# Attention with a causal mask, 1 core: the second key block masked by GpSimd on the probabilities, its PV one slot later

## The chip, the cores and the metric

One Trainium2 chip, one core. The metric is the device time of one launch in microseconds. The engines are TensorE (PE; its weight loads are PEld), VectorE (DVE), ScalarE (ACT), GpSimd (POOL) and SyncE (SP, which issues DMAs).

## The reference

```python
xn = _layernorm(x)                         # x: 32 x 256 x 128, float32
x = x + attention_block(xn) + expert_layer(xn)
# in the attention block, 16 heads of 8:
scores = jnp.einsum('bhse,bhte->bhst', Q, K) * scale
scores = jnp.where(causal[None, None], scores, -1000000000.0)
attn = jax.nn.softmax(scores, axis=-1)
ctx = jnp.einsum('bhst,bhtd->bhsd', attn, V)
```

The attention block goes on with a low-rank output projection, a residual, a second layer norm and a low-rank GELU MLP. The expert layer routes each token to 2 of 9 experts (SiLU gate, width 352). Only the causal mask and the product with V are touched by the change.

## The kernel before

**Stages.** 8192 tokens are 16 chunks of 512, which is 2 sequences of 256 each. A first stage loads and normalises x and makes the router's logits. The second stage, 16 steps of attention, one chunk in each, runs from about 86 us to 588 us of the span. The third stage does the experts and the MLP. The change is in the second.

**A step.** Each engine has its own `step(half, d)`, an order written out by hand over 24 slots (`2 * UNITS`, `UNITS` = 12). A slot does one score unit. Slots 0 to 11 are the chunk's first sequence (b = 0), 12 to 23 the second (b = 1). In a half chunk, units u = 0 to 7 are the scores of the first 128 keys against 256 queries, 2 heads in each, and units 8 to 11 those of the last 128 keys against the last 128 queries, 4 heads in each; both are 128 keys on the partitions by 512 columns. The first keys against the last queries need no mask; the diagonal blocks do.

**A slot.** PE makes the scores with one matmul (`score_unit`, L1057), whose contraction has a 97th row: the negated row maximum of each query is in the stacked queries, so the result is already score minus maximum. A second matmul (L1058) adds `mask_ts` (0 or -1e30) to the diagonal blocks through the identity: 256 columns in units 0 to 7, all 512 in units 8 to 11. It ends with `scores_done`. ACT takes the exp of it (`exp_unit`, L846) from PSUM into one of 8 SBUF buffers `probs` and ends with `exp_done`. PE then multiplies two units' probabilities with V (`probs_times_v`, called PV below; L1075 for units below 8, L1082 for the others); PV number n takes units 2n and 2n + 1, 12 of them in a chunk. In each slot PE also does one max unit (`max_unit`, L1034 and L1037): the same scores with queries on the partitions, for a later half chunk, of which DVE takes the row maxima (L1441).

**The row maxima's way.** In slot 9 (for b = 1) and in slot 21 (for the next chunk's b = 0) PE turns the maxima (`turn_max`, L1090), ACT negates them into `neg_max` (`copy_max`, L839), and SP puts them by DMA into the 97th row of the stacked queries (`stack_max`, L486). The score of slot 12, or of slot 0 of the next chunk, is the first that reads them, and PE waits there:

```python
if u == 0:
    pe.wait_ge(max_stacked[b], 16 * (c.index + 1))
```

**Where PV stands.** In slots 3, 5, ... 23 PE does PV 0 to 10 after the slot's score and mask; PV 11 comes in slot 1 of the next chunk. In each slot the order is: score, mask, PV if any, the other small products (projections of q, k and v in slots 12, 14 and 2, the context's turns and output projection in 6, 8, 10, 18, 20, 22, the turn of the maxima in 9 and 21), then the max unit. After the last chunk PV 11 stands alone.

**POOL.** Its `step` goes over 12 pairs of slots. In pair k it waits until the scores of slot 2k are done (`after_scores`) and then issues, as the case may be, one row scatter of 128 tokens by an indirect DMA (L664; from chunk 3 on, in pairs 0 to 9, from chunk 11 on in pairs 0 to 11), a part of the key stack (L626; pairs 1 to 3 and 8 to 10), expert weights (pairs 0 and 6, eight chunks), and in pair 7 the output bias onto xn (L649). In the last chunk it also splits expert weights (L704). POOL doesn't take part in the scores.

**Buffers.** Two PSUM banks take the scores in turn: the score of slot m waits for the exp of slot m - 2. The exp of an even slot m waits for the PV that read the same `probs` buffers 8 units before.

Of the kernel before, what the change touches and what calls it, by code (L numbers as in the profile page):

```python
# [34 lines left out]
P = 128  # L35
# [24 lines left out]
def at(half, d):  # L60

    return Step(2 * half + d, d % 2, half + d // 2)
# [99 lines left out]
def first_and_attention(nc, env):  # L162
# [18 lines left out]
    with ExitStack() as stack:  # L181
# [160 lines left out]
        max_scores, max_taken = s.sem("max_scores"), s.sem("max_taken")  # L342
        max_turned, max_copied = s.sem("max_turned"), s.sem("max_copied")
        max_stacked = s.two_sems("max_stacked")
        scores_done, exp_done = s.sem("scores_done"), s.sem("exp_done")
        pv_done, ctx_copied = s.sem("pv_done"), s.sem("ctx_copied")
        ctx_back, inv_ready, ctx_ready = s.sem("ctx_back"), s.sem("inv_ready"), s.sem("ctx_ready")
        ctx_again, ctx_turned_ready = s.sem("ctx_again"), s.sem("ctx_turned_ready")
# [32 lines left out]
        def scatter_at(step, pair):  # L381

            if pair < ROWS_OF.get(step, 0):
                j = ROWS_AT[step] + pair
                return j // (2 * TPC), j % (2 * TPC)
            return None

        def fill_at(step, pair):

            if pair < 2 * TPC and step < LATE:  # L390
                k = 2 * TPC * step + pair
                return k if k < FILLS else None
            return None
# [13 lines left out]
        SPLIT_PAIRS = range(1, 1 + EXPERTS)  # L407
        SPLIT_SLOTS = range(4, 4 + 2 * EXPERTS, 2)
        HALVES = 2 * UNITS // 2


        Q_AT, K_AT, V_AT = (1, 9), (2, 10), 4
# [12 lines left out]
        with nc.Block() as block:  # L425
# [138 lines left out]
            def _(pool):  # L564
# [97 lines left out]
                def scatter(c, col):  # L662
                    t, k = divmod(col, 2)
                    pool.indirect_dma_start(env["slot_x"][:], bass.IndirectOffsetOnAxis(ap=slot_now[c.parity][:, col:col + 1], axis=0),  # L664
                                            xs[c.parity][:, t, k, :], None).then_inc(scattered[c.parity], 16)

                def after_scores(p, slot):
                    pool.wait_ge(scores_done, 2 * UNITS * p.index + slot)
                    pool.sem_inc(scatter_started, 1)

                def step(half, d):
                    p = at(half, d)
                    x = p.index
                    last = x == last_chunk
                    two_ahead = x < last_chunk - 1
                    for pair in range(HALVES):
                        after_scores(p, 2 * pair + 1)
                        rows, blank_part, weights = scatter_at(x, pair), fill_at(x, pair), weights_at(x, pair)
                        if x == LATE and pair == 0:
                            pool.wait_ge(slots_ready, 1)  # L680
                            pool.wait_ge(zero_filled, 16 * FILLS)
                            pool.wait_ge(routed_all, 1)
                        if rows is not None:
                            if rows[1] == 0:
                                number_rows(at(0, rows[0]))
                            scatter(at(0, rows[0]), rows[1])
                        if blank_part is not None:
                            fill(blank_part)
                        if pair == BIAS_AT:
                            add_bias(p)  # L690
                        if pair in K_SECOND_AT and not last:
                            stack_k_part(at(half, d + 1), 1, K_SECOND_AT.index(pair))
                        if pair in K_FIRST_AT and two_ahead:
                            if pair == K_FIRST_AT[0]:
                                pool.wait_ge(k_split, x + 3)
                                pool.sem_inc(k_stack_started, 1)
                            stack_k_part(at(half, d + 2), 0, K_FIRST_AT.index(pair))
                        if weights is not None:
                            load_weights(weights)
                        if last and pair in SPLIT_PAIRS:  # L700
                            pool.wait_ge(experts_loaded, 16 * W_LOADS)
                            pool.sem_inc(scatter_started, 1)
                            e = SPLIT_PAIRS.index(pair)
                            pool.tensor_copy(w_hi[:, e, :], w_gate_up[:, e, :].bitcast(F32)).then_inc(w_hi_ready, 1)  # L704
# [201 lines left out]
            def _(pe):  # L906
# [133 lines left out]
                def score_unit(c, m):  # L1040
# [13 lines left out]
                        g = u - 8  # L1054
                        keys, queries, lanes = k[rows, g, hi:end], slice(hi, end), slice(0, LANES)
                    by_lane = ps[:].rearrange("p (i s) -> p i s", s=queries.stop - queries.start)
                    pe.matmul(by_lane, keys, q[rows, g, lanes, queries], start=True, stop=False, skip_group_check=True)  # L1057
                    pe.matmul(by_lane[:, :, 0:P], ident_b[:], mask_ts[:, lanes, :], start=False, stop=True, skip_group_check=True).then_inc(scores_done, 1)  # L1058

                def probs_times_v(c, n):  # L1060

                    b, u = divmod(n, HALVES // 2)
                    seq = 2 * c.index + b
                    pe.wait_ge(exp_done, 2 * UNITS * c.index + 2 * (n + 1))
                    if n == 0:
                        pe.wait_ge(v_ready, c.index + 1)
                    if u == 0 and seq == 3:
# [48 lines left out]
                def step(half, d):  # L1116
# [4 lines left out]
                    before, here = 2 * x - 1, 2 * x  # L1121
                    for slot in range(2 * UNITS):
                        score_unit(p, slot)
                        if slot % 2 == 1 and slot >= 3:
                            probs_times_v(p, (slot - 3) // 2)
                        if slot == 1 and not first:
                            probs_times_v(at(half, d - 1), HALVES - 1)
                        if slot == 2 and not last:
                            project_v(nxt, bank_of(0, d), max_copied, 2 * x + 1)
                        if slot == COUNT_AT and x == 1:  # L1130
# [87 lines left out]
                step(chunks // 2 - 2, 1)  # L1218
                step(chunks // 2 - 1, 0)
                step(chunks // 2 - 1, 1)  # L1220
                probs_times_v(at(chunks // 2 - 1, 1), HALVES - 1)
                end = 2 * chunks - 1
                keep_busy(m_ps[0], 3)
                context_back(end, bank_of(1, 2), h_done, end)
# [862 lines left out]
```

## Time and profile before

| | us |
|---|---|
| median of 3 runs | 999.45 |
| lowest, highest | 994.67, 1008.21 |
| the profiled execution | 1002.02 |
| its span, first to last instruction | 1000.1 |
| mean granted TensorE clock in it | 0.982 |

The durations in the profile are from that one execution; the difference between 1002.02 and 1000.1 lies around the span. A matmul's row gives its start and a modelled end, and matmuls are pipelined, so what one costs PE is read from the starts, its own and the next one's. A PEld row is a weight load, which overlaps the matmul before it. The text in brackets behind a row is the idle time of that engine ahead of it and what ended it.

### The profile page before, as it was taken

The numbers are of one execution on the slowest core, as the hardware profiler recorded it, in microseconds if no ns is written. First come the engines' busy times: TensorE is split into PE (matmuls) and PEld (weight loads), VectorE is DVE, ScalarE is ACT, GpSimd is POOL, SyncE is SP. The second block draws the span as 40 slices with busy tenths as digits, with TensorE's granted clock in tenths as the row PEclk, the third lists the DMA queues.
The fourth block names the chain that finished last, engine by engine and source line by source line (L and its number), as shares of the span: only waits on it lengthen the run. The fifth ranks groups of instructions, "written<-read, shape, count | busy, mean of one in ns | idle before, by whom it ended". The sixth has DMA issues, their size and how long they took to land. (4 is left out here: it accounts for less than half of the span.)

```text
span 1000.1 us, 25308 instructions
## 1 busy us (share of the span) xinstructions
PE 956.2 (96%) x7722; PEld 742.4 (74%) x7722; DVE 698.5 (70%) x3195; ACT 533.9 (53%) x1248; POOL 428.1 (43%) x557
## 2 busy tenths in 40 slices
PE   4689999999999999999999989999999999999997
PEld 4455666666666666666666659999999999989896
DVE  5768889778777777777777745555555554558887
ACT  2663555555555555555555555555555555564442
POOL 9331221354645556454555425444444444430110
PEclk8779999999999999999999999999999999999999
DMA  9477453444554454443433032222222222248874
GB/s 243 126 233 228 164 206 110 136 137 132 156 150 131 126 151 141 130 121 105 134 107 121 30 90 72 66 66 62 66 64 65 65 65 65 73 135 232 230 214 135
DMA packets 139765, 127.12 MB, mean 127 GB/s; under 512 B 17338, under 2 KB 121908, under 8 KB 139636
## 3 DMA queue, kind: packets, MB, share of 16 engines
q1 hardware_dynamic: 116336, 68.94, 25.4%
q0 software_dynamic: 20592, 56.43, 18.0%
q8 instruction: 67, 1.10, 0.5%
q10 hardware_dynamic: 2708, 0.15, 0.2%
q14 instruction: 62, 0.51, 0.2%
HBM read 57.15 MB, written 42.60 MB: 100 GB/s over the span
## 5 line engine op out<-in xcount | busy, mean ns | idle before, releaser
L1441 DVE CUSTOM_DVE_ANT_0 att_masked_st<-att_m_ps,att_mask_st 128x128 bf16<-128x128 f32 (+1 forms) x1024 | 311.4, 353 | 100.1 <-PE att_m_ps L1034 52.1
L846 ACT ACTIVATE att_probs<-att_t_ps 128x512 f32<-128x512 f32 x384 | 229.0, 597 | 206.2 <-PE att_t_ps L1058 201.0
L1683 POOL DMA_INDIRECT y_scratch<-moe_y,moe_row_now x136 | 131.6, 968 | 153.8 <-DVE moe_y L1937 112.6
L664 POOL DMA_INDIRECT slot_x<-xs,att_slot_now x128 | 127.7, 998 | 151.3 <-PE att_t_ps L1058 128.4
L1931 DVE TENSOR_TENSOR moe_hidden<-moe_gate,moe_up_ps 128x352 f32<-128x352 f32 x136 | 70.9, 521 | 109.8 <-ACT moe_gate L1858 108.1
L1058 PE MATMUL att_t_ps<-att_mask_ts,att_ident_b 128*128 128x256 bf16 (+1 forms) x384 | 122.9, 320 | 0.0
L1760 PE MATMUL moe_y_ps<-w_down,moe_hidden_t 128*128 (+1 forms) x816 | 114.0, 276 | 1.7 <-DVE moe_y L1937 1.5
L1858 ACT ACTIVATE moe_gate<-moe_gate_ps 128x352 f32<-128x352 f32 x136 | 63.1, 464 | 97.2 <-PE moe_up_ps L1743 97.2
L1760 PEld LDWEIGHTS moe_y_ps<-w_down,moe_hidden_t 128*128 128x128 f32 (+1 forms) x816 | 101.8, 191 | 3.5 <-issue 3.2
L1441 DVE DVE_READ_ACCUMULATOR2_ANT att_row_max<- 128x1 f32 x1024 | 84.5, 83 | 0.1
L1057 PE MATMUL att_t_ps<-even_stack,att_k_stack 97*128 97x512 f32 x192 | 80.5, 419 | 3.6 <-DMA even_stack<-att_neg_max 3.2
L1057 PE MATMUL att_t_ps<-att_odd_stack,att_k_stack 97*128 97x512 f32 x192 | 80.9, 423 | 2.4 <-DMA att_odd_stack<-att_neg_max 2.4
L1058 PEld LDWEIGHTS att_t_ps<-att_mask_ts,att_ident_b 128*128 128x128 bf16 x384 | 37.3, 97 | 60.4 <-issue 52.1
L1075 PE MATMUL att_pv_ps<-att_probs,att_v_ones 128*32 128x256 f32 x1024 | 81.8, 391 | 0.0
L626 POOL DMA_DIRECT2D att_k_stack<-att_qk_parts x96 | 55.8, 581 | 30.9 <-PE att_t_ps L1058 28.4
L1034 PE MATMUL att_m_ps<-att_k_stack,even_stack 96*128 96x256 f32 x256 | 66.6, 342 | 2.4 <-DMA even_stack<-att_qk_parts 1.4
L1752 PE MATMUL moe_hidden_ps<-ident,moe_hidden 128*128 128x128 f32 (+1 forms) x408 | 66.7, 272 | 0.0
L1034 PE MATMUL att_m_ps<-att_k_stack,att_odd_stack 96*128 96x256 f32 x256 | 65.1, 336 | 0.6 <-DVE att_row_max L1441 0.6
L1743 PE MATMUL moe_gate_ps<-even_stack,moe_x_lo 128*128 x136 | 55.6, 409 | 0.7 <-DVE moe_x_lo L1925 0.7
L1034 PEld LDWEIGHTS att_m_ps<-att_k_stack,even_stack 96*128 96x128 f32 x256 | 40.0, 193 | 20.9 <-issue 18.1
L1852 ACT CAST moe_x_hi<-moe_x_ps 128x128 fp32r<-128x128 f32 x136 | 36.1, 267 | 33.2 <-PE moe_x_ps L1724 33.2
L1752 PEld LDWEIGHTS moe_hidden_ps<-ident,moe_hidden 128*128 128x128 f32 (+1 forms) x408 | 51.0, 136 | 2.9 <-issue 0.2
(268 smaller groups left out, 2053.6 us busy)
## 6 DMA issues: line engine op xcount, KB each, us to landing
att_k_stack<-att_qk_parts POOLq DMA_DIRECT2D x96, 128.0 KB, 3.3
slot_x<-xs POOLq DMA_DIRECT2D x17, 516.0 KB, 3.5
xs<-slot_x SPq DMA_DIRECT2D x34, 258.0 KB, 3.0
xs<-xn_scratch SPq DMA_DIRECT2D x32, 256.0 KB
mlp_rows<-y_scratch POOLq DMA_DIRECT2D x16, 512.0 KB, 5.4
even_stack<-att_qk_parts SPq DMA_DIRECT2D x192, 32.0 KB
att_odd_stack<-att_qk_parts SPq DMA_DIRECT2D x192, 32.0 KB
first_words<-in_L_attn_hidden_states SPq DMA_DIRECT2D x8, 512.0 KB, 7.9
```

The source lines that it names most:

```text
L664: pool.indirect_dma_start(env["slot_x"][:], bass.IndirectOffsetOnAxis(ap=slot_now[c.parity][:, col:col + 1], axis=0), xs[c.parity][:, t, k ...
L846: act.activation(probs[:, m % PT, :], t_ps[m % 2][:], ACT.Exp).then_inc(exp_done, 1)
L1034: last = pe.matmul(ps[:, n * SEQ:(n + 1) * SEQ], q[0:ROWS, g, i, hi:hi + P], k[0:ROWS, g, lo:lo + SEQ], start=True, stop=True)
L1057: pe.matmul(by_lane, keys, q[rows, g, lanes, queries], start=True, stop=False, skip_group_check=True)
L1058: pe.matmul(by_lane[:, :, 0:P], ident_b[:], mask_ts[:, lanes, :], start=False, stop=True, skip_group_check=True).then_inc(scores_done, 1)
L1075: last = pe.matmul(pv_ps[b][32 * i:32 * i + 32, at_col:at_col + SEQ], v_ones[c.parity][:, 2 * b, head_of(u, i), :], pt, start=(u == 0), st ...
L1441: last = dve.tensor_tensor_reduce(out=masked_st[m % 2][:, part], in0=m_ps[m % 2][:, part], in1=mask_st[:, SEQ - width:], scale=1.0, scalar ...
L1683: pool.indirect_dma_start(env["y_dram"][:], bass.IndirectOffsetOnAxis(ap=row_now[q.parity][:, t:t + 1], axis=0), y[c.parity][:], None).the ...
L1752: last = pe.transpose(hidden_ps[0:n, k * P:(k + 1) * P], hidden[c.parity][:, col:col + n], ident[:])
L1760: last = pe.matmul(y_ps[:, 0:P], hidden_t[c.parity][0:n, k * P:(k + 1) * P], down_cols[0:n, ds(e * (NCH * P) + k * P, P)], start=(k == 0), ...
L1858: act.activation(gate[c.parity][:], gate_ps[c.parity][:, 0:FF], ACT.Silu).then_inc(gate_done, 1)
L1931: dve.tensor_tensor(hidden[c.parity][:], gate[c.parity][:], up_ps[c.parity][:, 0:FF], ALU.mult).then_inc(hidden_done, 1)
```

## The change

`score_unit` leaves out the mask's matmul for units 8 to 11; their scores go to exp unmasked. On POOL, in the pairs of slots 8 and 9, 10 and 11, 20 and 21, 22 and 23, a new function `keep_causal` waits for the exp of each of the two slots and sets to 0, in place in `probs`, what lies above the diagonal. It stands ahead of the pair's DMA issues. The PV of these units waits for POOL's new semaphore `causal_done` and no longer for `exp_done`. PV 4, 5, 10 and 11 move from slots 11, 13, 23 and 1 of the next chunk to slots 12, 14, 0 of the next chunk and 2 of the next chunk; all others stay. After the last chunk two PVs stand alone.

```diff
@@ constants
+        PV_AT = {3: 0, 5: 1, 7: 2, 9: 3, 12: 4, 14: 5, 15: 6, 17: 7, 19: 8, 21: 9}
+        PV_BEHIND = {0: 10, 2: 11}
@@ POOL
+                def keep_causal(c, m):
+
+                    pool.wait_ge(exp_done, 2 * UNITS * c.index + m + 1)
+                    unit = probs[:, m % PT, :].rearrange("p (i s) -> p i s", i=LANES)
+                    pool.affine_select(out=unit, in_=unit, compare_op=ALU.is_ge, fill=0.0, base=0,
+                                       pattern=[[0, LANES], [1, P]], channel_multiplier=-1).then_inc(causal_done, 1)
+
                 def after_scores(p, slot):
...
                         rows, blank_part, weights = scatter_at(x, pair), fill_at(x, pair), weights_at(x, pair)
+                        if 2 * pair % UNITS >= 2 * GROUPS:
+                            keep_causal(p, 2 * pair)
+                            keep_causal(p, 2 * pair + 1)
@@ PE, score_unit
-                    pe.matmul(by_lane, keys, q[rows, g, lanes, queries], start=True, stop=False, skip_group_check=True)
-                    pe.matmul(by_lane[:, :, 0:P], ident_b[:], mask_ts[:, lanes, :], start=False, stop=True, skip_group_check=True).then_inc(scores_done, 1)
+                    last = pe.matmul(by_lane, keys, q[rows, g, lanes, queries], start=True, stop=(u >= 8), skip_group_check=True)
+                    if u < 8:
+                        last = pe.matmul(by_lane[:, :, 0:P], ident_b[:], mask_ts[:, lanes, :], start=False, stop=True, skip_group_check=True)
+                    last.then_inc(scores_done, 1)
@@ PE, probs_times_v
-                    pe.wait_ge(exp_done, 2 * UNITS * c.index + 2 * (n + 1))
+                    if u < GROUPS:
+                        pe.wait_ge(exp_done, 2 * UNITS * c.index + 2 * (n + 1))
+                    else:
+                        pe.wait_ge(causal_done, GROUPS * (2 * c.index + b) + 2 * (u - GROUPS + 1))
@@ PE, step
-                        if slot % 2 == 1 and slot >= 3:
-                            probs_times_v(p, (slot - 3) // 2)
-                        if slot == 1 and not first:
-                            probs_times_v(at(half, d - 1), HALVES - 1)
+                        if slot in PV_AT:
+                            probs_times_v(p, PV_AT[slot])
+                        if slot in PV_BEHIND and not first:
+                            probs_times_v(at(half, d - 1), PV_BEHIND[slot])
@@ PE, after the last chunk
-                probs_times_v(at(chunks // 2 - 1, 1), HALVES - 1)
+                for n in PV_BEHIND.values():
+                    probs_times_v(at(chunks // 2 - 1, 1), n)
```

## Rows read from the trace of the kernel before

**Rows 1.** The page, busy time, share of the span and instructions

```profile
PE 956.2 (96%) x7722; PEld 742.4 (74%) x7722; DVE 698.5 (70%) x3195; ACT 533.9 (53%) x1248; POOL 428.1 (43%) x557
```

**Rows 2.** Busy time by stretch: PE, PEld, DVE, ACT, POOL, clock, DMA, GB/s

```profile
300.00:350.00 50.00, 49.35 (x441) 32.08 (x437) 38.06 (x227) 27.96 (x51) 25.82 (x34) 1.00 0.46 128
```

**Rows 3.** Timeline, PE, slots 20 to 23, then 0 and 1: start, us, instruction

```profile
400.64 0.39 PE L1058 MATMUL att_t_ps<-att_mask_ts,att_ident_b 128*128 128x512 bf16 x1
400.87 0.38 PE L1106 MATMUL att_free_ps<-ident,att_ctx 128*128 128x128 f32 x2
...
402.46 0.39 PE L1090 MATMUL att_free_ps<-ident,att_row_max 128*16 128x128 f32 x2
...
404.08 0.40 PE L1057 MATMUL att_t_ps<-att_odd_stack,att_k_stack 97*128 97x512 f32 x1
404.33 0.39 PE L1058 MATMUL att_t_ps<-att_mask_ts,att_ident_b 128*128 128x512 bf16 x1
404.65 0.65 PE L1082 MATMUL att_pv_ps<-att_probs,att_v_ones 128*32 128x128 f32 x16
405.22 0.50 PE L1034 MATMUL att_m_ps<-att_k_stack,even_stack 96*128 96x256 f32 x2
405.56 0.40 PE L1057 MATMUL att_t_ps<-even_stack,att_k_stack 97*128 97x512 f32 x1
405.81 0.28 PE L1058 MATMUL att_t_ps<-att_mask_ts,att_ident_b 128*128 128x256 bf16 x1
405.85 0.48 PE L1034 MATMUL att_m_ps<-att_k_stack,even_stack 96*128 96x256 f32 x2
...
406.41 0.29 PE L1058 MATMUL att_t_ps<-att_mask_ts,att_ident_b 128*128 128x256 bf16 x1
406.62 0.64 PE L1082 MATMUL att_pv_ps<-att_probs,att_v_ones 128*32 128x128 f32 x16
```

**Rows 4.** Timeline, ACT and SP's queue, of the same slots 20 to 22

```profile
401.07 0.60 ACT L846 ACTIVATE att_probs<-att_t_ps 128x512 f32<-128x512 f32 x1 [0.86 <-PE att_t_ps L1058]
...
402.00 0.60 ACT L846 ACTIVATE att_probs<-att_t_ps 128x512 f32<-128x512 f32 x1
402.88 0.37 ACT L839 ACTIVATE att_neg_max<-att_free_ps 16x256 fp32r<-16x256 f32 x1 [0.29 <-PE att_free_ps L1090]
...
403.28 0.55 SPq L486 DMA_DIRECT2D even_stack<-att_neg_max  x1
```

**Rows 5.** The tile neg_max: who waited for it (us, times), DMA to landing

```profile
  PEld att_t_ps L1057: 8.7, 14
...
DMA to landing us min/median/max: 2.1/2.1/3.4
```

**Rows 6.** Timeline, PE and its loads, slots 12 and 13 of another chunk

```profile
326.48 0.19 PEld L1057 LDWEIGHTS att_t_ps<-att_odd_stack,att_k_stack 97*128 97x128 f32 x1 [0.79 <-DMA att_odd_stack<-att_neg_max]
...
326.83 0.28 PE L1058 MATMUL att_t_ps<-att_mask_ts,att_ident_b 128*128 128x256 bf16 x1
326.95 1.02 PE L1008 MATMUL att_free_ps<-att_xt,wq 128*128 128x512 f32 x2
...
328.05 0.39 PE L1057 MATMUL att_t_ps<-att_odd_stack,att_k_stack 97*128 97x512 f32 x1
```

**Rows 7.** Groups by line and shape, PE, 84 to 590 us: busy, mean ns

```profile
L1058 PE MATMUL att_t_ps<-att_mask_ts,att_ident_b 128*128 128x512 bf16 x128 | 50.1, 392 | 0.0
```

**Rows 8.** Groups by line and shape, POOL, whole span

```profile
L664 POOL DMA_INDIRECT slot_x<-xs,att_slot_now x128 | 127.7, 998 | 151.3 <-PE att_t_ps L1058 128.4 <-issue 22.9
L626 POOL DMA_DIRECT2D att_k_stack<-att_qk_parts x96 | 55.8, 581 | 30.9 <-PE att_t_ps L1058 28.4 <-DVE att_qk_parts L1418 1.8 <-issue 0.4
L649 POOL TENSOR_TENSOR att_xn_both<-att_xn_both,out_bias 128x512 f32<-128x512 f32 x16 | 20.7, 1293 | 11.8 <-PE att_t_ps L1058 11.5
...
L596 POOL TENSOR_SCALAR_AFFINE_SELECT att_mask_ts<-att_mask_ts 128x512 bf16<-128x512 bf16 x1 | 0.6, 631 | 0.0
...
L594 POOL TENSOR_SCALAR_AFFINE_SELECT att_mask_st<-att_mask_st 128x256 f32<-128x256 f32 x1 | 0.4, 396 | 0.0
```

More of the change, by code:

```diff
@@ L344, in first_and_attention @@
         max_stacked = s.two_sems("max_stacked")
-        scores_done, exp_done = s.sem("scores_done"), s.sem("exp_done")
+        scores_done, exp_done, causal_done = s.sem("scores_done"), s.sem("exp_done"), s.sem("causal_done")
         pv_done, ctx_copied = s.sem("pv_done"), s.sem("ctx_copied")
```

## The prediction

> **What bounds the kernel now.** I first read the busy times: TensorE (PE) is busy 96% of the span, DVE 70%, ACT 53%, POOL 43% [rows 1]. The change touches the attention steps alone, so I read a stretch of them by itself: in 50 us there PE is busy 49.35, DVE 38.06, ACT 27.96, POOL 25.82, at the full granted clock (1.00, which is the 2.4 GHz level) [rows 2]. So what PE loses in work is time won, as long as PE isn't made to wait.
>
> Next I looked for the places where PE does wait, in the timeline around one half chunk's end. PE turns the row maxima (L1090) in slot 21, ACT negates them (L839) 0.42 us later, SP issues their DMA into the stack (L486) 0.82 us after the turn, and the first score of the next half chunk (L1057, slot 0; likewise turn in slot 9, score in slot 12) can't start before this DMA has landed [rows 3, 4]. PE needs from 402.46 to 405.56 = 3.10 us for what lies between the two [rows 3]. The DMA lands 2.1 us after its issue at the least and at the median, 3.4 at most [rows 5], so the chain takes 0.82 + 2.1 = 2.92 us. **Only 0.18 us lie between the two.** In 14 of the 31 such windows the chain already ends last: the weight load of L1057 waits 8.7 us in total [rows 5]; one of them is the score at 326.48, whose load waited 0.79 us [rows 6]. In the other 17, PE's own work ends last.
>
> **The change, part by part.**
>
> *Masks removed.* 128 matmuls with 512 columns go (8 for each of 16 chunks) [rows 7]. Their 392 ns are with pipelining; the cost is in the starts. From the mask's start to the next matmul's it is 0.23 us (400.64 to 400.87), from the score's start to the mask's 0.25 (404.08 to 404.33) [rows 3]. I take 0.24, bounds 0.23 and 0.25: 128 x 0.24 = 30.7 us gross. The Trainium skill, "TensorE: Matmul & The Clock Gate" (Wait — 56ns, not 53.3ns?), gives N / 2.4 GHz plus 2.5 ns from start to start, 216 ns for 512 columns; by it the gross would be 27.6 us (an estimate from that page). The rows here lie above it.
>
> *Which of them count.* Per half chunk two masks lie ahead of the turn (slots 8 and 9, or 20 and 21) and two inside the window. Those ahead bring everything later forward: 31 half chunks x 2 x 0.24 = **14.9 us won**.
>
> *The window.* Inside it PE loses the mask of slot 22 (0.24) and the mask and PV of slot 23 (404.33 to 405.22 = 0.89) [rows 3]: 3.10 - 0.24 - 0.89 = 1.97 us of work. The chain stays at 2.92, since the turn, ACT's copy, SP's issue and the DMA are untouched. So the 17 windows that PE ended shrink by 0.18 only, **3.1 us won**, and the other 14 by nothing. PE stands still for about 0.95 us in every window.
>
> *PV one slot later.* The fifth PV of a half chunk was in slot 11 or 23, inside the window, where 17 times it filled it and 14 times it cost nothing. It moves to slot 12 or 0, behind the score that waits, where PE has no slack. Before slot 0's next matmul it puts 0.21 + 0.57 us (406.41 to 406.62, 404.65 to 405.22) in place of 0.04 (405.81 to 405.85), +0.74; in slot 12 in place of 0.12 (326.83 to 326.95), +0.66 [rows 3, 6]. Mean 0.70 x 31 = **21.7 us lost**. The sixth PV moves from slot 13 or 1 to 14 or 2, from ahead of a max unit to ahead of a projection, which by the same rows is 0.08 cheaper: 2.5 us won.
>
> *The selects.* POOL gets 128 of them, 128x512 f32. The nearest rows: 396 ns for 128x256 f32, and 631 ns for 128x512 bf16 [rows 8]. I take 0.63 us; the lower bound is that row too, as columns and not bytes seem to count, the upper is the two-input add on 128x512 f32, 1.29 us [rows 8]. 128 x 0.63 = 81 us more on POOL, which is idle half of these 500 us [rows 2]. In time: the exp of slot 21 ends at 402.60, 0.14 us after the turn, that of slot 20 at 401.67 [rows 4]. Even one behind the other from 402.60, both selects end 1.4 us after the turn; the PV behind the waiting score comes 2.92 + 0.3 us after it. Behind the selects on POOL stand a scatter issue (1.00 us and up to 0.9 to start), in the second half a k-stack issue (0.58), and the next two selects. In slot 14 the sixth PV is due about 6.2 us after the turn, in slot 2 about 5.4 (2.92, then slot 12 with 326.48 to 328.05 = 1.57 and 0.66 more, slot 13 without its PV some 0.6, and 0.46 to the PV; slot 0 is 0.9 shorter) [rows 3, 6]; the selects end by 4.6 and, where the scatter and the k-stack both stand before them (4 chunks), by 5.1. The probabilities' 8 buffers hold: a PV is needed 8 units later. So selects cost PE nothing; at 1.29 us each those 4 chunks would lose about 2 us. The scatters get later by 1.3 us at most per pair of pairs; SP loads their rows behind the stack's DMA or long before it.
>
> *Last half chunk.* It has no window behind it. Its 4 masks give up to 1.0 us, its last select (0.3 to 1.3 us between the last exp and the last PV) takes as much. Zero.
>
> **Sum.** -14.9 - 3.1 + 21.7 - 2.5 = **+1.2 us**. Against the profiled execution's own 1002.02 that is 1003.2; the median of the runs before is 999.45, within whose spread (994.67 to 1008.21) the profiled one lies, so I forecast 999.45 + 1.2 = 1001 us. What is to be learned: 30.7 us of PE work go and the time stays, since half the masks were inside a window that a DMA closes, and the moved PV leaves that window.
>
> **The rivals.**
>
> *A, the whole gain (faster).* The window would not bind, and PE work would be all: 999.45 - 30.7 = 969 us. For it speaks PE's busy share. Against it: the landing would have to come 1.97 - 0.82 = 1.15 us after the issue, and its least is 2.1 [rows 5]. 6%.
>
> *B, the landing gets longer (slower).* Place: L486 to L1057. Before, 17 windows had 0.18 us of cover; now none has any, so each 0.1 us on the mean landing costs 31 x 0.1 = 3.1 us. The scatters of slots 8 and 20 are now issued behind two selects, which moves their packets toward this DMA's flight. From +0.65 us on the mean it is over 2% with the sum; at +0.8 us the time is 999.45 + 1.2 + 25 = 1025. For it: landings reach 3.4 us. Against it: the median is at the minimum although 128 scatters run in these steps [rows 5, 8]. 10%.
>
> *C, POOL ends late (slower).* If a select with its start takes 1.6 us, the sixth PV waits: four selects from 0.8 us ahead of the turn, 1.8 us of scatter between, against 6.2 us, decides from 1.3 us a select. At 1.6 it is 1.2 us x 31 = 37 us, 1038. The Trainium skill, "GPSIMD Engine Reference" (Engine selection; Key points), speaks for it: elementwise work belongs on VectorE, and GpSimd shares SBUF interfaces with VectorE and contends with its two-input instructions. Against it stand 631 ns, and the add's 1.29 us as the mean of 16 in steps in which DVE is busy 38 of 50 us [rows 2, 8]. 7%.
>
> A change that doesn't do what it says I see no room for: the mask's matmul is left out at build time.
>
> **Numbers.** Forecast 77% (its own range 990 to 1013, from the mask's 0.23 to 0.25, a landing 0.2 us either way where it can go, and the runs' own spread), A 6%, B 10%, C 7%. About 2% (20 us) is what a measurement of this kernel can tell from no change. Of the forecast 2% lie below 979.5. Faster 0.08, same 0.75, slower 0.17. The range for 8 in 10 is 985 to 1025: it reaches B's price and part of the way to A.
>
> **What would show it.** In the changed kernel's profile, L1057 waits for the DMA of neg_max in all 31 windows rather than 14, by some 0.95 us in the 17 and 1.1 more than before in the 14, about 39 us in total against 8.7; from L1090 to the waiting L1057 it takes 2.9 us in most windows; PE's busy share in the attention falls to about 93%, the clock stays 1.00 (a stall of 0.79 us stands in a stretch with 1.00 now [rows 2, 6]). The selects take about 0.63 us, and no PV waits for POOL. I am wrong if PE is still busy throughout while the time falls (A), if L486's landing has a median well over 2.1 (B), or if L1082 waits for POOL (C).

## The result, and the profile after

The changed kernel takes 1035.62 us in the median of 4 runs (1031.71 to 1039.44), the kernel before 999.87 in the same comparison. The ratio is 1.0364, with a 95% interval of 1.0328 to 1.04: slower by 3.6%, where I had forecast no change and ranged to 1025. The profiled execution took 1031.71, its span is 1029.8 us against 1000.1, and its mean granted TensorE clock 0.967 against 0.982.

The page's busy times, as in [rows 1]:

```profile
PE 951.7 (92%) x7594; PEld 743.1 (72%) x7594; DVE 695.1 (68%) x3195; ACT 531.9 (52%) x1248; POOL 510.9 (50%) x685
```

PE has 128 matmuls less, but only 4.5 us less busy time: what it does takes longer. By stretch of the attention steps (columns as in [rows 2]; the clock is the third from the end):

```profile
75.00:100.00 25.00, 21.51 (x138) 13.49 (x136) 22.53 (x135) 7.83 (x14) 7.82 (x13) 0.97 0.64 214
100.00:125.00 25.00, 23.62 (x196) 14.62 (x194) 18.42 (x95) 11.90 (x21) 8.31 (x13) 0.90 0.38 141
125.00:150.00 25.00, 23.10 (x181) 14.93 (x178) 17.80 (x108) 11.82 (x23) 9.11 (x14) 0.93 0.59 203
150.00:200.00 50.00, 45.23 (x399) 29.09 (x398) 41.51 (x229) 25.62 (x47) 18.98 (x29) 1.00 0.37 112
200.00:250.00 50.00, 46.58 (x399) 30.07 (x397) 36.39 (x218) 26.94 (x49) 33.41 (x46) 0.97 0.47 135
250.00:300.00 50.00, 45.81 (x392) 30.43 (x388) 33.51 (x199) 24.62 (x46) 30.80 (x42) 0.93 0.44 126
300.00:350.00 50.00, 46.60 (x399) 30.08 (x397) 35.80 (x213) 26.67 (x49) 33.52 (x45) 0.97 0.44 126
350.00:400.00 50.00, 45.68 (x389) 30.11 (x386) 34.77 (x208) 25.39 (x47) 30.54 (x44) 0.93 0.47 133
400.00:450.00 50.00, 46.62 (x405) 30.60 (x404) 35.20 (x210) 26.27 (x48) 32.22 (x44) 0.97 0.44 126
450.00:500.00 50.00, 46.59 (x403) 30.28 (x400) 36.28 (x217) 26.74 (x49) 31.72 (x43) 0.97 0.38 107
500.00:550.00 50.00, 47.50 (x418) 31.25 (x422) 36.40 (x219) 27.18 (x51) 34.35 (x47) 1.00 0.42 123
550.00:600.00 50.00, 47.21 (x436) 31.19 (x432) 38.23 (x242) 27.53 (x51) 31.43 (x43) 1.00 0.26 78
```

Two things are to be seen. PE's busy time is about 46.5 of 50 us, where it was 49.35: it stands still. And the clock is under 1.00 in nine of the twelve stretches. At its low level of 1.2 GHz it counts half, so the time spent there is twice what is missing: 2 x (25 x 0.20 + 50 x 0.26) = 36 us. The kernel before has no such time from 75 to 550 us.

The wait for the row maxima's DMA, as in [rows 5]:

```profile
  PEld att_t_ps L1069: 43.0, 31
...
DMA to landing us min/median/max: 2.1/2.1/3.4
```

All 31 windows now end with the DMA, 43.0 us in total; the prediction had 39. The median of the landing looks as it was, but it mixes two kinds of window. One ahead of slot 12, with the clock at 1.00, for comparison with [rows 3, 6] (PE, then ACT, SP's queue and POOL in the same stretch):

```profile
541.03 0.39 PE L1107 MATMUL att_free_ps<-ident,att_row_max 128*16 128x128 f32 x2
...
544.02 0.50 PE L1069 MATMUL att_t_ps<-att_odd_stack,att_k_stack 97*128 97x512 f32 x1 [0.83 <-DMA att_odd_stack<-att_neg_max]
544.36 0.28 PE L1071 MATMUL att_t_ps<-att_mask_ts,att_ident_b 128*128 128x256 bf16 x1
544.57 0.64 PE L1099 MATMUL att_pv_ps<-att_probs,att_v_ones 128*32 128x128 f32 x16
545.15 1.12 PE L1020 MATMUL att_free_ps<-att_xt,wq 128*128 128x512 f32 x2
```

```profile
541.46 0.37 ACT L851 ACTIVATE att_neg_max<-att_free_ps 16x256 fp32r<-16x256 f32 x1 [0.21 <-PE att_free_ps L1107]
541.86 0.56 SPq L488 DMA_DIRECT2D att_odd_stack<-att_neg_max  x1
...
543.10 1.23 POOL L673 TENSOR_SCALAR_AFFINE_SELECT att_probs<-att_probs 128x512 f32<-128x512 f32 x2
```

From the turn to the waiting score it is 2.99 us, as the chain gives, and the PV (L1099) is then done behind it. The next PE rows also show a size that I had missed: from the score that waited to its mask it is 0.34 us (544.02 to 544.36), where it is 0.24 or 0.25 without a wait [rows 3]. Its weight load can't lie under an earlier matmul.

The selects, by tile (min/median/max ns):

```profile
L673 POOL TENSOR_SCALAR_AFFINE_SELECT att_probs<-att_probs x128: 624/634/1277, 94.5 to 615.8; 128x512 f32<-128x512 f32 x128
```

634 ns, as forecast from the bf16 row of [rows 8]. In the 16 steps no PV waits for a select. The two PVs behind the last chunk do, 0.18 and 0.56 us; the second of them:

```profile
616.49 0.64 PE L1099 MATMUL att_pv_ps<-att_probs,att_v_ones 128*32 128x128 f32 x16 [0.56 <-POOL att_probs L673]
```

The other kind of window lies ahead of slot 0. In its slot 21 GpSimd issues a part of the key stack, a DMA of 128 KB. In the kernel before this came 1.63 us ahead of the maxima's DMA in most of these windows (401.65 and 403.28 in one, the latter in [rows 4]):

```profile
401.65 0.58 POOL L626 DMA_DIRECT2D att_k_stack<-att_qk_parts  x1 [0.71 <-PE att_t_ps L1058]
```

In the changed kernel it stands behind two selects and comes at the same moment (PE, SP's queue, POOL):

```profile
356.94 0.39 PE L1107 MATMUL att_free_ps<-ident,att_row_max 128*16 128x128 f32 x2
...
357.76 0.56 SPq L488 DMA_DIRECT2D even_stack<-att_neg_max  x1
357.80 0.62 POOL L628 DMA_DIRECT2D att_k_stack<-att_qk_parts  x1
```

The score that waits starts 3.11 us after SP's issue, where it is 2.16 in the window above (541.86 to 544.02). So it goes in all 11 windows in which the two issues lie within 0.1 us of each other: the landing's median is 3.0 us there, from 2.85 to 3.4, where it was 2.13 ahead of slot 0 before. In the three later ones in which a scatter too stands before the key stack's issue, so that this comes 1.25 us behind the maxima's, it is 2.13. Ahead of slot 12 the median is 2.13. The 2.1 of [rows 5] was taken from 16 DMAs, the ones whose landing that profile tells: 15 of them are those ahead of slot 0.

The end of that window is also a fall of the clock (PE's timeline; the granted clock is 0.57 in the stretch from 361 to 365 us and 1.00 in that from 350 to 361, in which PE was busy for 9.23 of 11.00 us):

```profile
360.87 0.50 PE L1069 MATMUL att_t_ps<-even_stack,att_k_stack 97*128 97x512 f32 x1 [1.77 <-DMA even_stack<-att_neg_max]
361.21 0.40 PE L1071 MATMUL att_t_ps<-att_mask_ts,att_ident_b 128*128 128x256 bf16 x1
361.54 1.08 PE L1099 MATMUL att_pv_ps<-att_probs,att_v_ones 128*32 128x128 f32 x16
362.55 0.80 PE L1046 MATMUL att_m_ps<-att_k_stack,even_stack 96*128 96x256 f32 x2
```

PE stood for 1.77 us, and then the same PV takes 1.01 us from its first start to the next matmul's (361.54 to 362.55), where at 2.4 GHz it is 0.58 (544.57 to 545.15). From 224 to 464 us the clock falls eight times, each time about 0.4 us behind the score that ended such a window ahead of slot 0, with stands of 1.68 to 1.77 us. The windows ahead of slot 12 between them, with stands of 0.82 to 0.87 us, bring no fall, and neither do the eight from 480 us to 591 us, with 0.81 to 0.90, as the key stack's issue comes later there. Two earlier stands, of 1.54 us at 157 and 2.12 at 192, brought none either.

### The profile page after: what moved, and what is told of

Same layout as the page of the kernel before. It is cut to its first block and busy times, and to the rows that moved or that the text cites. A ratio compares the mean times of both kernels' runs of the same rounds, so it can differ in the third digit from the quotient of the medians.

```text
span 1029.8 us, 25180 instructions
## 1 busy us (share of the span) xinstructions
PE 951.7 (92%) x7594; PEld 743.1 (72%) x7594; DVE 695.1 (68%) x3195; ACT 531.9 (52%) x1248; POOL 510.9 (50%) x685
## 5 line engine op out<-in xcount | busy, mean ns | idle before, releaser
L1459 DVE CUSTOM_DVE_ANT_0 att_masked_st<-att_m_ps,att_mask_st 128x128 bf16<-128x128 f32 (+1 forms) x1024 | 307.7, 353 | 136.0 <-PE att_m_ps L1046 73.6
L673 POOL TENSOR_SCALAR_AFFINE_SELECT att_probs<-att_probs 128x512 f32<-128x512 f32 x128 | 83.6, 662 | 39.3 <-ACT att_probs L858 18.8
L1069 PE MATMUL att_t_ps<-att_odd_stack,att_k_stack 97*128 97x512 f32 x192 | 84.0, 439 | 20.0 <-DMA att_odd_stack<-att_neg_max 20.0
L1069 PE MATMUL att_t_ps<-even_stack,att_k_stack 97*128 97x512 f32 x192 | 83.6, 435 | 16.8 <-DMA even_stack<-att_neg_max 16.8
L1071 PE MATMUL att_t_ps<-att_mask_ts,att_ident_b 128*128 128x256 bf16 x256 | 75.4, 295 | 0.0
L1046 PE MATMUL att_m_ps<-att_k_stack,even_stack 96*128 96x256 f32 x256 | 69.5, 355 | 2.1 <-DMA even_stack<-att_qk_parts 1.0
L1046 PE MATMUL att_m_ps<-att_k_stack,att_odd_stack 96*128 96x256 f32 x256 | 68.4, 350 | 2.6 <-DVE att_row_max L1459 2.4
L1046 PEld LDWEIGHTS att_m_ps<-att_k_stack,att_odd_stack 96*128 96x128 f32 x256 | 41.5, 201 | 21.7 <-issue 13.4
L1046 PEld LDWEIGHTS att_m_ps<-att_k_stack,even_stack 96*128 96x128 f32 x256 | 42.2, 202 | 20.6 <-issue 14.7
L1071 PEld LDWEIGHTS att_t_ps<-att_mask_ts,att_ident_b 128*128 128x128 bf16 x256 | 25.7, 100 | 42.8 <-issue 33.6
```

Source lines behind the costliest of these rows:

```text
L673: pool.affine_select(out=unit, in_=unit, compare_op=ALU.is_ge, fill=0.0, base=0, pattern=[[0, LANES], [1, P]], channel_multiplier=-1).then ...
L1046: last = pe.matmul(ps[:, n * SEQ:(n + 1) * SEQ], q[0:ROWS, g, i, hi:hi + P], k[0:ROWS, g, lo:lo + SEQ], start=True, stop=True)
L1069: last = pe.matmul(by_lane, keys, q[rows, g, lanes, queries], start=True, stop=(u >= 8), skip_group_check=True)
L1071: last = pe.matmul(by_lane[:, :, 0:P], ident_b[:], mask_ts[:, lanes, :], start=False, stop=True, skip_group_check=True)
L1459: last = dve.tensor_tensor_reduce(out=masked_st[m % 2][:, part], in0=m_ps[m % 2][:, part], in1=mask_st[:, SEQ - width:], scale=1.0, scalar ...
```

## The experiments

All ran against the kernel before. My first theory after the result: two losses that add up, the PV behind the wait, and the clock, which falls because PE stands. Rival: GpSimd's selects.

**1. The changed kernel with the stand filled.**

```diff
@@ PE, score_unit
                     if u == 0:
+                        keep_busy(ps, 3)
                         pe.wait_ge(max_stacked[b], 16 * (c.index + 1))
```

(The wait for the exp of two slots before now stands ahead of it. `keep_busy` multiplies constants into a PSUM bank, here the one that the score overwrites.)

> The changed kernel, and in slots 0 and 12 PE does three dummy products (512 columns each) into the score's own bank before it waits for the row maxima's DMA. Theory (the clock): in the changed kernel PE stands still about 1 us in each of 31 windows, and its granted clock falls to 1.2 GHz for 37 us of the attention, which costs half of that, 19 us. The dummies fill 0.7 us of the stand, so the clock holds at 0.98 and the time is 1035.6 - 19 = 1017 (1010 to 1023). Rival (GpSimd's selects slow the steps, through waits or contention): the dummies help nothing, 1035 or more. Rival (the stands themselves and the moved PV are all): also 1035.

1020.51 us (1019.92 to 1021.82), ratio 1.0208 [1.0175, 1.024]: 15 us less than the changed kernel, though PE does 96 products more. The granted clock is 0.986, and by stretch:

```profile
350.00:400.00 50.00, 47.71 (x423) 31.30 (x422) 35.66 (x218) 26.51 (x50) 32.51 (x45) 1.00 0.49 142
300.00:350.00 50.00, 47.69 (x416) 30.36 (x412) 36.13 (x215) 27.27 (x50) 33.96 (x46) 1.00 0.44 128
```

The attention steps have no fall left. So the falls come from the stands, and cost some 15 us. The selects are all still there, at the same place, and the landings ahead of slot 0 are as long as in the changed kernel (median 2.97 us); what changed is that PE now stands there for 1.0 to 1.15 us in a row in most of them, where it was 1.7.

**2. The PV moved, nothing else.**

```diff
@@ PE, step (kernel before)
-                        if slot % 2 == 1 and slot >= 3:
-                            probs_times_v(p, (slot - 3) // 2)
-                        if slot == 1 and not first:
-                            probs_times_v(at(half, d - 1), HALVES - 1)
+                        if slot in PV_AT:                       # {..., 12: 4, 14: 5, ...}
+                            probs_times_v(p, PV_AT[slot])
+                        if slot in PV_BEHIND and not first:     # {0: 10, 2: 11}
+                            probs_times_v(at(half, d - 1), PV_BEHIND[slot])
```

> The kernel before, with the PV of the last four units one slot later alone: all masks on PE, no select. Theory (PV leaves a window that the DMA closes): work in the window falls from 3.10 to about 2.5 us, the DMA closes it at 3.0, and the PV behind the wait costs 0.83 us in slots 0 and 12 by the changed kernel's starts: 31 x (0.83 - 0.1) = +22, 1022 us (1015 to 1030). L1057's loads wait in 31 of 31 windows, 0.5 us more each. Rival (the selects are the cause): 1000 us, as before.

1022.61 us (1022.42 to 1025.71), ratio 1.0225 [1.0194, 1.0257]. PE's timeline at a window's end, and the tile of the maxima:

```profile
402.13 0.50 PE L1059 MATMUL att_t_ps<-att_odd_stack,att_k_stack 97*128 97x512 f32 x1 [0.48 <-DMA att_odd_stack<-att_neg_max]
402.47 0.28 PE L1060 MATMUL att_t_ps<-att_mask_ts,att_ident_b 128*128 128x256 bf16 x1
```

```profile
  PEld att_t_ps L1059: 25.9, 31
```

Moving one PV of each half chunk by one slot, over the wait, costs 23 us without a select and without one mask less. With stands of half a microsecond the clock held (0.980); its one fall in the steps after the first two chunks, at 554 us, stands behind a stand of 1.27 us. Here the key stack's issue keeps its 1.6 us ahead of the maxima's, and the landing ahead of slot 0 its 2.1 us.

**3. The masks taken away, nothing else.**

```diff
@@ PE, score_unit (kernel before)
-                    pe.matmul(by_lane, keys, ..., start=True, stop=False, ...)
-                    pe.matmul(by_lane[:, :, 0:P], ident_b[:], mask_ts[:, lanes, :], ...).then_inc(scores_done, 1)
+                    last = pe.matmul(by_lane, keys, ..., start=True, stop=(u >= 8), ...)
+                    if u < 8:
+                        last = pe.matmul(by_lane[:, :, 0:P], ident_b[:], mask_ts[:, lanes, :], ...)
+                    last.then_inc(scores_done, 1)
```

> The kernel before without the mask's matmul of units 8 to 11 and without any select; PV in its old slots. The second key block stays unmasked. Theory (windows closed by the DMA): 2 x 0.23 us less per half chunk ahead of the turn, and only 0.1 of the other 0.47 in the window: 31 x 0.56 = 17 us less, 983 us (978 to 988); the loads wait in all 31 windows, about 0.35 us more each; the clock holds. Rival (PE's work alone counts): 30 us less, 970.

993.22 us (991.98 to 997.19), ratio 0.9934 [0.9902, 0.9967]: 30 us of PE work less bring 6. That is even less than my window theory said. From the starts of the 31 windows, their mean length is 3.39 us where it was 3.31; and outside them a half chunk is 0.31 us shorter, not 0.46.

```profile
  PEld att_t_ps L1057: 25.2, 29
...
DMA to landing us min/median/max: 2.1/2.2/4.1
```

The fence has the waits of the maxima's tile and its DMA's landing (min/median/max). 29 windows wait now. Each wait lays the weight load of the score that waited bare (0.10 us), and the longest landing has grown from 3.4 to 4.1. The landing ahead of slot 0 has gone from 2.13 to 2.69 us in the median, without any select: two masks less ahead of the turn bring the maxima's issue closer to the key stack's, which most of these windows now have 1.40 us ahead of it and no longer 1.63. Of the 11 us that are missing, the windows make 5.6 (31 times 3.39 in place of 3.21).

**4. Selects and no masks, but PV in its old slots.**

```diff
-        PV_AT = {3: 0, 5: 1, 7: 2, 9: 3, 12: 4, 14: 5, 15: 6, 17: 7, 19: 8, 21: 9}
-        PV_BEHIND = {0: 10, 2: 11}
+        PV_AT = {3: 0, 5: 1, 7: 2, 9: 3, 11: 4, 13: 5, 15: 6, 17: 7, 19: 8, 21: 9, 23: 10}
+        PV_BEHIND = {1: 11}
```

> The changed kernel with its selects on GpSimd, but PV in its old slots (5th in 11 and 23, 6th in 13 and 1). Theory (the move was the loss, not the select): the 5th PV fills the window again. Its select is done about 1.0 us after the turn, and PE comes to it about then, so that little is waited: 983 to 992 us, clock 0.98. Rival (the selects are the loss, so the PV waits on GpSimd in slots 11, 13, 23 and 1): 1015 or more, with loads of L1099 waiting for the select.

998.91 us (993.4 to 1004.57), ratio 1.0006 [0.9982, 1.0031]: the time of the kernel before. The move was the loss, as the theory said; the gain that I expected beside it is not there. The selects cost 5.7 us against experiment 3, of which 1.7 lie behind the last score (9.95 us from it to the first expert product, where it is 8.27 without selects). The timeline of a window at a chunk's end (SP's queue, POOL, PE):

```profile
401.46 0.55 SPq L488 DMA_DIRECT2D even_stack<-att_neg_max  x1
401.50 0.61 POOL L628 DMA_DIRECT2D att_k_stack<-att_qk_parts  x1
...
404.49 0.50 PE L1069 MATMUL att_t_ps<-even_stack,att_k_stack 97*128 97x512 f32 x1 [1.07 <-DMA even_stack<-att_neg_max]
```

The key stack's issue comes at the same moment as the maxima's, as in the changed kernel, and the score starts 3.03 us after SP's issue. PE stands there for 1.07 us, as the PV fills the rest.

**5. The changed kernel without the selects** (`keep_causal` isn't called, PV waits for the exp).

> The changed kernel without the selects: PV in the new slots waits for the exp, the second key block stays unmasked. Theory (the selects only add what they add with PV in the old slots, 998.9 - 993.2 = 5.7 us, by delaying GpSimd's DMA issues into the flight of the row maxima's DMA): 1030 us (1025 to 1035), the clock falls as in the changed kernel. Rival (the selects bring the clock's falls about): 1015, clock 0.98.

1026.23 us (1024.43 to 1032.88), ratio 1.0261 [1.0201, 1.0322]; clock 0.970. The falls are there without any select: five after the first two chunks, each behind a stand of 1.3 to 1.9 us at this DMA. What the selects add to the changed kernel is about 1%.

**6. The kernel before with the turn one slot earlier.**

```diff
@@ PE, step; the same in ACT's step for copy_max
-                        if slot == 9:
+                        if slot == 8:
                             ... turn_max(p, 1, ...)
-                        if slot == 21 and not last:
+                        if slot == 20 and not last:
                             turn_max(nxt, 0, ...)
```

> The kernel before, with PE's turn of the row maxima and ACT's copy of them in slots 8 and 20 rather than 9 and 21, nothing else. Theory (the DMA closes the window): the chain starts about 1.4 us earlier, so nearly no load of L1057 waits; the mean window was 3.31 us with 3.10 of work: 31 x 0.21 = 6.5 us less, 992 us. Rival (the wait goes to another place, as the turn itself waits for its maxima or its bank): 999.

1000.26 us (996.47 to 1007.74), ratio 0.9999 [0.997, 1.0028]. The loads' waits fell from 8.7 us in 14 windows to 4.9 in 5, and the time stayed. The turn now stands behind another small transpose instead of behind PV:

```profile
404.27 0.38 PE L1106 MATMUL att_free_ps<-ident,att_ctx 128*128 128x128 f32 x2
404.49 0.38 PE L1090 MATMUL att_free_ps<-ident,att_row_max 128*16 128x128 f32 x2
404.63 0.48 PE L1034 MATMUL att_m_ps<-att_k_stack,even_stack 96*128 96x256 f32 x2
```

From L1106 to L1034 it is 0.36 us there against 0.14 + 0.14 in two places before. Over slots 8 and 9 the median is 2.60 us against 2.51: 0.09 a half chunk, which eats most of what the stands gave (0.12). So this wait was not worth what I had put on it.

**7. The same move in the changed kernel.**

> The changed kernel with the turn and the copy of the row maxima in slots 8 and 20. Theory: the starts of the changed kernel, stands taken out, give 29.9 us of PE work per chunk against 31.84 before: 15.5 x 1.94 = 30 less, 1.7 more at the end, 971 us (966 to 978); the clock holds. That is 64 us under the changed kernel. Rival (GpSimd or the moved PV are the loss by themselves): over 1000.

1008.2 us (999.37 to 1018.98), ratio 1.0066 [1.0036, 1.0097]. It takes most of the loss back, 27 us, but not the 64 that I expected. The expectation had set the work of one kernel against the mean of the other, 31.84 us a chunk, which holds stands and odd slots: the medians of the 24 slots add up to 31.2 before and to 30.3 here. The waits are down to 12.3 us in 10 windows. The profiled execution took 1018.98 us, with the clock at 0.965. Of its five falls after the first two chunks three come at a stand of 1.8 to 2.3 us at this DMA, and two behind a stand at another place, a max unit that waits for DVE's row maxima:

```profile
479.08 1.11 PE L1049 MATMUL att_m_ps<-att_k_stack,even_stack 96*128 96x128 f32 x4 [1.20 <-DVE att_row_max L1459]
```

**8. Old slots for PV and the turn early.**

> The selects on GpSimd and the masks off PE, PV in its old slots, and the turn and copy of the row maxima in slots 8 and 20. Theory: 8 masks of 0.235 us less per chunk and no stands, 15.5 x 2.3 = 36 less, 1 more at the end: 965 us (958 to 972); by the turn of the changed kernel's selects the PV's data is there 0.5 us before PE comes. Rival (the move was needed, since PV now waits for its select): L1099 waits in slots 11 and 23, above 975.

993.9 us (990.54 to 1000.36), ratio 0.993 [0.9904, 0.9957]: faster than the kernel before, by a fifth of what I expected.

Who waited for the maxima's tile (us, times), and under it what is to be read from the slots:

```profile
  PEld att_t_ps L1069: 10.2, 11
```

The medians of the 24 slots add up to 29.8 us a chunk, against 31.2 before; from one slot 0 to the next it is 31.2 in the mean, against 31.8. So single slots far over the median (waits for this DMA of up to 3.1 us in slots 11 and 23, and the low clock) take more than half of the gain.

**9. The selects behind the pair's DMA issues,** in the changed kernel and in experiment 4.

```diff
@@ POOL, step
-                        if 2 * pair % UNITS >= 2 * GROUPS:
-                            keep_causal(p, 2 * pair)
-                            keep_causal(p, 2 * pair + 1)
                         if x == LATE and pair == 0:
...
+                        if 2 * pair % UNITS >= 2 * GROUPS:
+                            keep_causal(p, 2 * pair)
+                            keep_causal(p, 2 * pair + 1)
                         if last and pair in SPLIT_PAIRS:
```

> The changed kernel with the selects of a pair behind the pair's DMA issues rather than ahead of them. Theory (selects delay the key stack's DMA issue into the flight of the row maxima's DMA, which makes the window at slots 23 and 0 longer; without selects it was 1026, with them 1035.6): the landing's median in the profile falls, slot 23 by some 0.3 us, and the time to 1027 to 1031. Rival (GpSimd's work as such disturbs): 1035.

1027.38 us (1023.81 to 1034.7), ratio 1.027 [1.0243, 1.0296]: the selects' 1% is gone, as without them. The key stack's issue is back at 1.40 us ahead of the maxima's, the landing ahead of slot 0 went from 2.98 to 2.66 us in the median (over both kinds of window together it did not fall), and the median of slot 23 from 2.45 to 2.13.

> Masks off PE, PV in its old slots, selects behind the pair's DMA issues. Theory (as in the run before this): 998.9 falls toward 993.2, the value without selects: 994. Rival (now the select comes late and the PV in slots 11 and 23 waits for it): 1000 or more.

1001.56 us (998.34 to 1005.58), ratio 1.0024 [1.0004, 1.0044]. Here the rival was right: no gain, and for its reason. Slot 11 is 1.78 us in the median against 1.63 in experiment 4, since its PV stands there and its selects now come behind a scatter. Who waited for the select (us, times), where it was 2.6 us in 6 loads in experiment 4:

```profile
  PEld att_pv_ps L1099: 15.8, 26
```

Slot 23 fell as hoped, from 2.47 to 2.12.

**10. The window filled by a PV that is ready.** From experiment 4:

```diff
-        PV_AT = {..., 7: 2, 9: 3, 11: 4, 13: 5, ..., 19: 8, 21: 9, 23: 10}
+        PV_AT = {..., 7: 2, 10: 3, 11: 4, 13: 5, ..., 19: 8, 22: 9, 23: 10}
@@ ACT, step
-                        if slot == 9:
+                        if slot == 8:
                             copy_max(p, 1, ...)
-                        if slot == 21 and x != last_chunk:
+                        if slot == 20 and x != last_chunk:
                             copy_max(...)
```

> Masks off PE, selects ahead of the DMA issues, 5th and 6th PV in their old slots, and the 4th PV of each half chunk (slots 9 and 21, ahead of the turn) moved into the window, to slots 10 and 22; ACT copies the maxima before the exp of slot 9 or 21. Theory (a window that a DMA closes takes 0.6 us of PE work for nothing): the turn comes 0.57 us earlier and PE's work up to the wait is 3.2 us against a chain of 3.0: the loads wait in few windows, 31 x 0.5 = 15 us less than the kernel without this move (998.9): 984 us (978 to 990), clock 0.98 or more. Rival (another wait takes its place, as it did with the turn one slot earlier): 994 or more.

993.95 us (990.97 to 996.8), ratio 0.9955 [0.9936, 0.9973]. It beats the kernel before, like experiment 8, but by half a per cent, not by the 1.5% expected. The maxima's tile:

```profile
  PEld att_t_ps L1069: 8.4, 11
...
DMA to landing us min/median/max: 2.1/2.3/4.3
```

The medians of the slots again add up to less (29.9 us a chunk) than the mean from one slot 0 to the next (31.1): 11 windows still wait, for landings of up to 4.3 us, and the clock falls at 291 and 369 us, at stands of 1.5 and 2.1 us.

**11. The same with the selects behind the DMA issues.**

> The same with the selects behind the pair's DMA issues. Theory: as little as the landing is then in the way, 982 to 986. Rival: the PV of slots 11 and 23 waits for its select, 990 or more.

1000.84 us (993.88 to 1002.47), ratio 1.0007 [0.9988, 1.0026]. The maxima's tile, and who waited for the select:

```profile
  PEld att_t_ps L1069: 13.4, 15
...
DMA to landing us min/median/max: 2.2/3.0/4.0
```

```profile
  PEld att_pv_ps L1099: 16.1, 36
```

The rival was right. The PV's loads wait 16.1 us for the select, where it is 5.1 in experiment 10, and slots 11 and 23 both grow from 1.25 to 1.78 us in the median. The landing too is longer, but the profile tells that of 16 of the 32 DMAs alone, 15 of them ahead of slot 0: their median is 3.0 us, where in experiment 10 it is 2.3. The key stack's issue (402.06 in one window) and the maxima's (402.79) lie 0.7 us apart here, and 1.8 us there. This can't be the main cause of the loss: ahead of slot 12 the key stack's issue has not moved, and slot 11 grows by as much as slot 23. The order that helped in the changed kernel harms here, as the PV is due before its select is done.

## Why the prediction was wrong, step by step

**Right.** The window closes with the DMA in all 31 cases (43.0 us of waits against 39 predicted). A mask's worth: slots 8, 9, 20 and 21 are 0.22 to 0.24 us shorter, 14.4 us for the 62 masks ahead of the turn, against 14.9. The select's 0.63 us. In the steps no PV waits for GpSimd. And the main point, that the masks' gain goes into the window and the moved PV is paid behind it (experiments 2 to 4). The Trainium skill, "TensorE: Matmul & The Clock Gate" (Wait — 56ns, not 53.3ns?), has 216 ns; the slots here give 0.22 to 0.24 us.

**The steps that failed** are two, and the second hangs on the first. The first is "The chain stays at 2.92, since the turn, ACT's copy, SP's issue and the DMA are untouched". The DMA was untouched, but its surroundings were not: the selects of slots 20 and 21 put off GpSimd's issue of the key stack from 1.63 us ahead of the maxima's issue to the same moment, and in these 11 windows the landing takes 3.0 us in place of 2.1 and PE stands for some 1.7 us rather than 0.95. That the landing follows the distance of the two issues is read from four kernels and from both kinds of window; no run moves this one issue alone.

The second is "the clock stays 1.00 (a stall of 0.79 us stands in a stretch with 1.00 now)". For the stands of this length it was right: those of 0.8 to 0.9 us bring no fall. The clock falls behind the long ones, for 36 us of the attention. At half speed this is 18 us if PE works throughout; shortening the stands to about 1 us gave 15 back (experiment 1). Without selects it falls as well (experiment 5), behind stands of 1.3 to 1.9 us: there the masks' removal had already brought the two issues nearer, to 1.40 us in the median. The page "TensorE: Matmul & The Clock Gate" of the Trainium skill has the rule (Why this matters for your kernels) that throughput drops in mid-kernel are avoided by leaving no long idle gaps between bursts of matmuls. By this trace gaps of 1.7 us were enough, eight times in a row.

**Terms of the sum that were mis-sized:**

| term | predicted, us | from the traces, us |
|---|---|---|
| masks ahead of the turn | -14.9 | -14.4 |
| window, turn to waiting score | -3.1 | +2.4 (mean 3.31 to 3.39, 31 times; ahead of slot 12 3.33 to 3.12, ahead of slot 0 3.30 to 3.68) |
| 5th PV behind the wait | +21.7 | +25.7 (slot 0 +0.81, slot 12 +0.85) |
| 6th PV | -2.5 | 0 (slots 1 and 2, 13 and 14: -0.77 and +0.78) |
| clock | 0 | +15 (experiment 1) to +18 |
| end of the attention | 0 | +1.7 (last score to first expert product) |

The slot values are medians over the chunks where the clock was at 2.4 GHz. The rows overlap a little, since a slow stretch also lengthens windows; they add up to 30 to 33 us, and the two profiled executions differ by 29.7. The 5th PV was too cheap because I took the start of a mask behind a score that had not waited; behind a wait it is 0.10 us later. The 6th was credited with a difference between neighbours that the slots don't show. The end of the attention was put at zero (its last select was to take what its masks give), but the two PVs behind the last chunk wait 0.7 us for their selects, and the stand at the stage's end grows from 1.4 to 2.6 us; in all kernels with selects it is 1.7 us longer from the last score on, in those without not at all.

**The rivals.** A (969) is out. B was right in part. Its place was right, and its mechanism in kind: GpSimd's DMA issues behind the selects move into this DMA's flight. It had the scatters in mind, where the key stack's DMA did it, and its price left out the clock. Its sign, a median well over 2.1, failed only since the median was taken over both kinds of window; ahead of slot 0 it is 2.98. C's number (1038) comes near the measured one, its mechanism doesn't: without the selects the kernel still takes 1026. Against the "GPSIMD Engine Reference" of the Trainium skill, which sends elementwise work to VectorE, GpSimd was fast enough in the changed kernel: 634 ns a select. What it cost there, 1%, it cost through the DMAs queued behind it (experiment 9) and at the stage's end (1.7 us). With the PV in its old slots the selects had to come first: behind the DMA issues they are late by 16 us of the PV's loads (experiments 9 and 11). The longest selects, up to 1277 ns, fit that page's contention with VectorE; no run here separates them.

By ratios the parts add up: the move +2.25%, the masks -0.7%, selects +0.7 to +1.0%, together +2.3 to +2.6%; the whole is +3.64%. The rest, 1.0 to 1.3%, is near what shortening the stands gives back (1.0364 to 1.0208 is 1.5%): only together do the parts make stands long enough for the clock to fall again and again.

**Open:** why some stands of 1.5 us and more bring no fall, and which of the DMAs in flight makes single landings take 4 us.

## What to carry to other kernels

Before taking work off the busiest engine, mark the points where it waits for a chain of other engines, and write down per stretch between them what is work and what is slack: here 0.18 us. Work that leaves such a stretch for a place behind the wait is paid twice. Where the change makes the engine stand, price the clock too, by a run with the stands filled; and an engine that issues DMAs moves other DMAs' landings when it gets something to do. Read a wait by its place in the step: one median over all landings said 2.1 us before and after, and hid that those ahead of slot 0 had changed.

## What the runs showed of the hardware

- A granted clock of 1.00 with stands of 0.5 us in nearly every half chunk of 16 us (experiment 2) and with stands of 0.8 to 0.9 us in eight half chunks in a row (changed kernel, 480 to 591 us); falls to 1.2 GHz, eight in a row and 36 us in all, each of the eight behind a stand of about 1.7 us.
- A matmul behind a semaphore wait starts its successor 0.10 us later than one whose weight load lay under the matmul before (0.34 against 0.24).
- A 16 KB DMA landed 2.13 us after its issue in the median with a 128 KB DMA of GpSimd issued 1.63 us ahead of it or 1.25 us behind it, in 2.65 to 2.7 with it 1.40 us ahead (experiments 9 and 3), and in 3.0 with both issued at the same moment (changed kernel).
- A select on 128x512 f32 in SBUF takes GpSimd 634 ns, the bf16 one 631: by columns, not by bytes.
